# A gated cross-attention block with experts: side work moved from ScalarE's PSUM ring to a two-bank slot of VectorE's ring

## The reference

```
x = x + tanh(g_xattn) * attention(layernorm(x), ctx)   # x 2048 x 256, ctx 1601 x 256, 8 heads of 4 dims
    q = xn Wq + bq; k = ctx Wk + bk; v = ctx Wv + bv    # 256 -> 32
    attn = softmax(q k^T * scale); o = attn v; return o Wo + bo
x = x + tanh(g_ffn) * experts(layernorm(x))             # 8 experts, each takes its 512 best rows
    scores = softmax(xn router_w + router_b); G, idx = top_k(scores.T, 512)
    y[idx] += G * (relu(xn[idx] w1 + b1) w2 + b2)       # 256 -> 1024 -> 256
```

## Time and profile before

| | |
|---|---|
| median of 3 runs | 588.16 us (587.49 to 588.36) |
| the profiled execution | 587.38 us, span 585.6 us |
| granted TensorE clock | 0.996 of full speed |
| busy share of the span | PE 94%, PEld 55%, DVE 76%, ACT 67%, POOL 37% |

### The profile page before, as it was taken

The page is one execution under the profiler, slowest core; times in us unless marked ns, Lnnn a source line. Parts: engine busy times, 40 slices in busy tenths (PEclk is TensorE's granted clock), DMA queues, the critical chain, the costliest instruction groups (busy, mean ns, idle before and its releaser), DMA issues.

```text
span 585.6 us, 12822 instructions
## 1 busy us (share of the span) xinstructions
PE 548.6 (94%) x5043; PEld 319.9 (55%) x5043; DVE 442.3 (76%) x811; ACT 390.1 (67%) x762; POOL 215.0 (37%) x205
## 2 busy tenths in 40 slices
PE   7798999999999999999999988899999999999994
PEld 4433333343343333433334444479889898898973
DVE  3889889987999878999895277655866858676541
ACT  2577778987789887898889820055665556565651
POOL 3058085001835017300184110231544625437234
PEclk9999999999999999999999999999999999999998
DMA  7700000000000000000000105113635646356123
GB/s 275 252 2 1 1 1 3 2 2 37 2 37 2 2 37 1 38 2 2 37 37 2 38 19 163 31 52 107 137 110 107 166 133 136 110 108 164 18 35 36
DMA packets 23808, 35.80 MB, mean 61 GB/s; under 512 B 3460, under 2 KB 16197, under 8 KB 23621
## 3 DMA queue, kind: packets, MB, share of 16 engines
q1 hardware_dynamic: 17604, 26.59, 14.0%
q0 software_dynamic: 6144, 8.39, 8.2%
HBM read 26.59 MB, written 8.39 MB: 60 GB/s over the span
## 4 chain that ended last, share of the span: by engine, by line
PE 69%; DVE 18%; issue 4%; ACT 4%; POOL 1%; DMA 1%; POOLq 0%; DVEq 0%; ACTq 0%; SPq 0%
PE ps L1744 15%; PE ps L1751 15%; PE ps L1515 12%; DVE mquart L1040 11%; PE ps L1481 7%; PE ps L1502 6%; PE ps L1411 2%; ACT probs L767 2%; PE ps L1372 2%; PE ps L1387 1%; PE ps L1722 1%; PE ps L1697 1%; ACT osb L666 1%; PE ps L1540 1%; POOL out L636 1%
## 5 line engine op out<-in xcount | busy, mean ns | idle before, releaser
L1040 DVE TENSOR_REDUCE mquart<-ps 128x2 f32<-128x802 f32 x256 | 240.3, 987 | 27.4 <-PE ps L1481 25.2
L767 ACT ACTIVATE probs<-ps 128x512 f32<-128x512 f32 (+1 forms) x416 | 223.4, 595 | 28.8 <-PE ps L1502 26.2
L1515 PE MATMUL ps<-probs,vp 128*32 128x256 f32 (+1 forms) x1664 | 132.7, 391 | 4.2 <-ACT osb L666 4.0
L1481 PE MATMUL ps<-kpad,qrows 64*128 64x401 bf16 x512 | 89.5, 337 | 6.8 <-DVE mquart L1040 6.4
L1502 PE MATMUL ps<-qfull,kpad 64*128 64x256 bf16 (+1 forms) x832 | 88.6, 272 | 1.6 <-ACT x L788 1.4
L1340 DVE TENSOR_TENSOR h1l<-hf,h1h 128x512 fp32r<-128x512 f32 x64 | 44.2, 691 | 56.2 <-ACT hf L892 54.3
L891 ACT ACTIVATE h1h<-ps,b1T 128x512 fp32r<-128x512 f32 x64 | 44.0, 687 | 54.1 <-PE ps L1744 52.3
L1751 PE MATMUL ps<-w2h,h1h 128*128 128x256 f32 x256 | 73.8, 288 | 2.1 <-DVE h1l L1340 1.5
L1751 PE MATMUL ps<-w2l,h1h 128*128 128x256 f32 x256 | 72.4, 283 | 0.0
L1751 PE MATMUL ps<-w2h,h1l 128*128 128x256 f32 x256 | 72.3, 282 | 0.0
L636 POOL DMA_INDIRECT out<-eo,idx_put x32 | 55.3, 1727 | 26.4 <-ACT eo L901 17.3
(11 more groups left out here) (200 smaller groups left out, 690.4 us busy)
## 6 DMA issues: line engine op xcount, KB each, us to landing
w1raw<-in_L_ffn_w SPq DMA_DIRECT2D x16, 512.0 KB, 4.9
w2raw<-in_L_ffn_w SPq DMA_DIRECT2D x16, 512.0 KB
xs<-in_x SPq DMA_DIRECT2D x4, 512.0 KB, 8.2
ctx_sb<-in_ctx SPq DMA_DIRECT2D x3, 512.0 KB, 6.3
out<-xs SPq DMA_DIRECT2D x3, 512.0 KB, 2.7
x_rows<-x SPq DMA_DIRECT2D x3, 512.0 KB, 2.6
b2b<-in_L_ffn_b SPq DMA_DIRECT2D x1, 1024.0 KB, 10.7
out<-xs SPq DMA_DIRECT2D x2, 256.0 KB, 2.0
```

What stands on the lines that cost most here:

```text
L767: nc.scalar.activation(out_p, ps[0:w, next_bank(), :], ACT.Exp, scale=float(SCALE)).then_inc(s_ex, 1)
L1040: nc.vector.tensor_reduce(mquart[:, u % 2, t, a, :, kq], ps[:, b:b + 2, 0:MAXW], AX.X, ALU.max).then_inc(s_mr, 1)
L1481: last = mm(ps[:, bank + b, 0:MAXW], qrows[band(b), g, q:q + P], kpad[band(b), g, a, lo:lo + MAXW], start=True, stop=True)
L1515: last = mm(ps[32 * hh:32 * hh + 32, PV, 0:UW], vp[0:w, kt, g, hh, :], probs[0:w, step % PROBS, hh, :], start=(kt == 0), stop=(kt == NKT - 1))
```

## The change

The output projection and the turns of both norms leave ACT's ring. PE takes one two-bank slot of DVE's ring for both halves, writes them one after the other at one key tile, and one ACT instruction over 1024 columns takes both. DVE skips the slot in its own count. `slot_bank` works out for ACT which slot it is. The statistics of the norms move to other key tiles. The wait of `add_wo` counts one take for a chunk in place of two.

```diff
-        XN_FIRST, XN_LATER, Q_AT = ((0, 7), (0, 9)), ((0, 0), (0, 3)), ((1, 3), (1, 7))
-        X2_AT, ROUTER_AT = ((2, 7), (2, 9)), ((2, 10), (3, 0))
+        XN_FIRST, XN_LATER, Q_AT = (0, 9), (0, 3), ((1, 3), (1, 7))
+        X2_AT, ROUTER_AT = (2, 9), ((2, 10), (3, 0))
...
-        LN1_AT = {(u, kt): (c, ts) for c, u in ((2, 1), (3, PER_CHUNK + 1)) for kt, ts in ((7, (0, 1)), (8, (2, 3)))}
-        LN1_DONE = {(1, 9): 2, (PER_CHUNK + 1, 9): 3}
-        LN2_AT = {3: (0, 1), 4: (2, 3)}
+        LN1_AT = {(1, 3): (2, (0, 1)), (1, 7): (2, (2, 3)), (PER_CHUNK, 3): (3, (0, 1)), (PER_CHUNK, 9): (3, (2, 3))}
+        LN1_DONE = {(1, 8): 2, (PER_CHUNK, 10): 3}
+        LN2_AT = {3: (0, 1), 7: (2, 3)}
...
+        def dve_slots(u, kt):
+            c, g, h, r = unit(u)
+            return [name for name, here in (("o", (r, kt) == O_THIS), ("o_last", c > 0 and (r, kt) == O_LAST),
+                                            ("wo", c > 0 and (r, kt) == WO_AT), ("xn", c + 1 < NC and (r, kt) == xn_at(c)),
+                                            ("x2", c > 0 and (r, kt) == X2_AT)) if here]
+
+        def slot_bank(u, kt, name):
+            sides = sum(len(dve_slots(v, k)) for v in range(u + 1) for k in range(NKT if v < u else kt))
+            return dve_bank(tiles_by(u, 2 * kt + 1) + sides + dve_slots(u, kt).index(name))
...
-                nc.scalar.activation(x2[:, odd:CT:2, :], ps[:, bank, :].rearrange("p (t d) -> p t d", d=D), ACT.Copy,
+                nc.scalar.activation(x2[:, :, :].rearrange("p (t o) d -> p o t d", o=2),
+                                     ps[:, bank:bank + 2, :].rearrange("p o (t d) -> p o t d", d=D), ACT.Copy,
                                      scale=tg[:, 0:1]).then_inc(s_wt, 1)
...
-            def take_X(c, k, bank):
-                act.wait_ge(s_X, KD * c + k + 1)
-                take(x2T[:, k, :], ps[:, bank, :], s_Xt)
+            def take_X(c, bank):
+                act.wait_ge(s_X, KD * (c + 1))
+                nc.scalar.activation(x2T[:, :, :], ps[:, bank:bank + KD, :], ACT.Copy).then_inc(s_Xt, KD)
...
+                    for name in dve_slots(u, kt):
+                        if name in ("wo", "xn", "x2"):
+                            next_bank()
...
-                    if c > 0 and (r, kt) == (1, 5):
+                    if c > 0 and (r, kt) == (1, 8):
                         ln2_aggr(c - 1)
...
-                        even = next_act((s_wt, 2 * (c - 1) + 1))
-                        wo(c - 1, range(CT), (even, next_act((s_wt, 2 * c))))
-                    if c + 1 < NC and (r, kt) in xn_at(c):
-                        k = xn_at(c).index((r, kt))
-                        transpose_xn(c + 1, k, next_act((s_Tt, KD * (c + 1) + k + 1)))
+                        even = next_dve((s_wt, c))
+                        wo(c - 1, range(CT), (even, even + 1))
+                    if c + 1 < NC and (r, kt) == xn_at(c):
+                        first = next_dve((s_Tt, KD * (c + 2)))
+                        for k in range(KD):
+                            transpose_xn(c + 1, k, first + k)
...
-                    if c > 0 and (r, kt) in X2_AT:
-                        k = X2_AT.index((r, kt))
-                        transpose_x2(c - 1, k, next_act((s_Xt, KD * (c - 1) + k + 1)))
+                    if c > 0 and (r, kt) == X2_AT:
+                        first = next_dve((s_Xt, KD * c))
+                        for k in range(KD):
+                            transpose_x2(c - 1, k, first + k)
```

More of the change, by code:

```diff
@@ L514, in add_wo @@
                 pool.wait_ge(s_xb, c + 1)
-                pool.wait_ge(s_wt, 2 * (c + 1))
+                pool.wait_ge(s_wt, c + 1)
                 rows = xs[:, CT * c:CT * c + CT, :]
@@ L781, in q_full, with scale_wo @@
                 take(qfull[:, g, UW * h:UW * h + UW], ps[:, next_bank(), 0:UW], s_qf)
-            def scale_wo(c, odd, bank):
+            def scale_wo(c, bank):
                 act.wait_ge(s_W, c + 1)
@@ L816, in take_L, with take_xn @@
                 take(lg[:, CT * c:CT * c + CT, :], ps[:, bank, 0:P].rearrange("p (t j) -> p t j", j=32)[:, :, 0:E], s_lgr)
-            def take_xn(c, k, bank):
-                act.wait_ge(s_T, KD * c + k + 1)
-                take(xnT[:, k, :], ps[:, bank, :], s_Tt)
+            def take_xn(c, bank):
+                act.wait_ge(s_T, KD * (c + 1))
+                nc.scalar.activation(xnT[:, :, :], ps[:, bank:bank + KD, :], ACT.Copy).then_inc(s_Tt, KD)
             q_full(0)
@@ L835, in _ @@
                     if c > 0 and (r, kt) == WO_AT:
-                        for odd in range(2):
-                            scale_wo(c - 1, odd, next_bank())
-                    if c + 1 < NC and (r, kt) in xn_at(c):
-                        take_xn(c + 1, xn_at(c).index((r, kt)), next_bank())
+                        scale_wo(c - 1, slot_bank(u, kt, "wo"))
+                    if c + 1 < NC and (r, kt) == xn_at(c):
+                        take_xn(c + 1, slot_bank(u, kt, "xn"))
                     if c + 1 < NC and (r, kt) in Q_AT:
@@ L843, in _ @@
                         qk_bias(n, k, "q", k, CW, next_bank(), s_Q, NG * (c + 1) + k + 1)
-                    if c > 0 and (r, kt) in X2_AT:
-                        take_X(c - 1, X2_AT.index((r, kt)), next_bank())
+                    if c > 0 and (r, kt) == X2_AT:
+                        take_X(c - 1, slot_bank(u, kt, "x2"))
                     if c > 0 and (r, kt) == ROUTER_AT[0]:
```

## The result

| | before | changed |
|---|---|---|
| median | 588.28 us (22 runs) | 587.43 us (22 runs) |
| ratio to before | | 0.9987, 95% interval 0.9981 to 0.9993 |
| profiled execution, span | 585.6 us | 586.8 us |
| from unit 0's first scores to the last exponential | 288.19 us | 287.61 us |

What follows compares the result with a forecast made beforehand. PE's order was taken to bound units with side work, DVE the plain units and unit 0. Terms -1.2 + 1.1 + 0.7 + 0.7 - 1.3 summed to 0.0; with 0.2 off, 588.0 us, range 585.5 to 590.4.

Steps and rivals of the forecast that it cites:

- projection, units 4, 8, 12: Key tile 9: PE's 0.72 us loss behind the projection ends, less a 0.13 slot wait and 0.2 lag; gain 0.4 each.
- first norm's turns, units 4 and 8: Key tile 3: PE stands 0.70 us for the slot ACT is reading; cost 1.88 in place of 1.33, 0.55 slower each.
- first norm's turns, unit 0: Key tile 9: DVE is the bound there and idles 0.68 us behind the turns, not given back; 0.7 slower.
- second norm's turns, units 6, 10, 14: Key tile 9: the router waits for the whole take, 0.15 us in units 6 and 10, 0.4 in 14; 0.7 slower.
- statistics: Moved into DVE's gaps or under cover, mainly in units 1, 5 and 9, they delay PE less; 1.3 us faster together.
- Units with side work are PE-bound: Except in unit 0, PE's own order bounds units with side work (18 to 20.6 us), so edits are priced by PE's stalls.
- the sign: Units 4 and 8 stay at 19.8 to 20.0 us, with PE idle about 0.7 before a maximum, ended by ACT's take.
- POOL's cover: Unit 13's aggregation reaches POOL some 4 us later, hidden by POOL's 7.5 us wait for the last maxima.
- Takes: ACT's single takes last 1.01 us for 1024 columns and 1.10 for the projection.
- the faster one: Whole kernel: PE's stalls are made up at later waits and the covers hold; -2.6 us, 585.5; chance 0.28.
- The slower one: Whole kernel: DVE's queue falls to one maximum and takes start late behind ACT's exponentials; +3.0 us, 591.2; chance 0.17.
- That the statistics give nothing: Rival: the time the statistics held up goes to the wait for a slot; 0 in place of -1.3, 589.3; chance 0.10.

Runs made afterwards that it cites:

- stats_only: The kernel before with only the statistics moved to their new key tiles; ratio to before 0.9967, attention part 286.87 us against 288.19.
- stats_back: The changed kernel with the statistics of both norms back at their old key tiles; ratio to before 1.0012, attention part 288.98 us.
- xn_at_2: The changed kernel with the first norm's turns of units 4 and 8 at key tile 2 instead of 3; ratio to before 0.9980, attention part 287.26 us.
- wo_split: Projection in the slot and statistics moved, turns as before, projection's matmuls bank by bank with two takes; ratio to the kernel before 0.9946, attention part 285.73 us.

## Why the prediction was right, and by which terms

The forecast was 588.0 in a range of 585.5 to 590.4, on the scale of a 588.16 median; measured were 587.43 beside 588.28. That is right in sum. By terms, from the units' lengths in the kernels with one part each:

| step | forecast, us | measured, us |
|---|---|---|
| projection, units 4, 8, 12 | -1.2 | -1.52 |
| first norm's turns, units 4 and 8 | +1.1 | +0.8 |
| first norm's turns, unit 0 | +0.7 | +0.3 |
| second norm's turns, units 6, 10, 14 | +0.7 | +1.2 |
| statistics | -1.3 | -1.32 |
| sum | 0.0 | -0.54 (changed kernel: -0.58) |

- **Units with side work are PE-bound**: right, but for key tile 8 of unit 14 (below). Unit 4 took 1.4 us of DVE work more or less without moving, and PE's stalls came out in the unit's length, less what waits behind them gave back.
- **Projection**: the mechanism was right, its size 0.1 a unit too small. I took 0.2 back for ACT's lag. It is there: key tile 11 goes from 1.39 to 1.70, where the second score pair waits for an exponential (the 0.70 at 282.66). But key tiles 9 and 12 are each 0.1 shorter; at key tile 9 the projection starts 1.07 us behind the scores (279.06 in unit 12), where it was 1.17, since it no longer has to find two of ACT's three banks free.
- **First norm, units 4 and 8**: key tiles 0 to 4 went from 7.19 to 7.74 us, the forecast +0.55. The two errors in it cancelled: eight transposes in a row hold PE for 1.03 and not 1.18, and the stall is 0.84, not 0.70, because ACT's take begins 1.19 after the first transpose, 0.16 later than PE goes on, where I had counted 0.03. What I left out is that key tiles 5 and 6 then get 0.13 back, where PE had waited for DVE. So the units stood at 19.70, just under the 19.8 to 20.0 that I had named as the sign.
- **First norm, unit 0**: DVE's hole is 0.57, against 0.68 forecast, and half of that reached the unit's end. I read the eight maxima of the earlier trace rows as a full DVE. They were not: the changed kernel reads seven in 6.38 us and five in 4.59, a new one each 0.90 us, where those eight took 0.95 each. The merged row hid places where a maximum came late, with 0.08 and 0.07 us of idle time that it doesn't print, the first of them behind the turn at key tile 7. Against one each 0.90 us they had cost 0.36 over the eight; the hole of now costs 0.65 by the same count, and the difference of 0.3 is what the unit lost. The changed kernel's rows, DVE's timeline at the end of unit 0:

```profile
56.90 6.38 DVE L1052 TENSOR_REDUCE mquart<-ps 128x2 f32<-128x802 f32 x7
63.85 0.99 DVE L1052 TENSOR_REDUCE mquart<-ps 128x2 f32<-128x802 f32 x1 [0.57 <-PE ps L1496]
65.28 4.59 DVE L1052 TENSOR_REDUCE mquart<-ps 128x2 f32<-128x802 f32 x5
```

- **Second norm**: the step that was most too small. The router's wait adds 0.4 to key tile 10 in units 6 and 10 where I had 0.15. PE goes on 1.03 after the first transpose and not 1.18, so it reaches the router that much earlier and waits that much longer for a take that ends at 2.2 either way (and it starts 0.15 behind the take's end, not 0.06); key tiles 7 to 9 are 0.17 shorter, which leaves 0.26 a unit. In unit 14 it adds 0.5, and 0.34 more come at key tile 8, where DVE, no longer held off by a turn at key tile 7, is the bound (PE waits 0.16 for it at 313.13); the forecast has nothing there. Both waits in unit 14:

```profile
313.13 0.34 PE L1496 MATMUL ps<-kpad,qrows 64*128 64x401 bf16 x2 [0.16 <-DVE mquart L1052]
314.87 1.09 PE L1562 MATMUL ps<-cst,x 128*128 128x128 f32 x8
317.23 0.64 PE L1578 MATMUL ps<-x2T,rw_pad 128*32 128x128 f32 x16 [0.37 <-ACT x2T L814]
316.06 1.02 ACT L814 ACTIVATE x2T<-ps 128x1024 f32<-128x1024 f32 x1 [0.57 <-PE ps L1562]
```

- **Statistics**: right in each unit: 0.4 in unit 1, 0.8 in unit 5, 0.16 in unit 9, 0 in units 4 and 13. POOL's cover held as well: its wait for the last maxima shrank from 7.5 to 2.9 us and is not gone.
- **Takes**: 1.02 and 1.11 us (1024 and 1115 ns), where my slope gave 1.01 and 1.10. An estimate from the figures of the Trainium skill ("ScalarE: Activation LUTs", section "What ACT_TABLE_LOAD costs") was 1.04 and 1.13; the measurement lies between, nearer the slope.
- **The rivals**: the faster one wanted most stalls made up; 0.13 a unit was. The slower one wanted ACT at exponentials when a side ends; ACT waited 0.56 and 0.73 for PE there, so it never came into play. That the statistics give nothing is refuted by stats_only and stats_back. One thing in the working doesn't hold: it says that the range reaches to both outer cases, but it ends at 590.4 and the slower case at 591.2.

The result is the balance of terms of up to 1.5 us, so its closeness says less than the table does, and part of it is luck: the first three terms were each 0.3 to 0.4 too high and the second norm's 0.5 too low.

What stays open: in xn_at_2 ACT's take began 1.46 after the first transpose in unit 8, and 1.18 in unit 4, with the same rows on PE before it; behind the last transpose's modelled end that is 0.37 against 0.09. With two takes both units start at 0.69. No run here tells why.

## What to carry to other kernels

Joining two takes into one instruction saves 0.06 us at a turn and 0.15 at the projection here, but makes the first half wait for the second; where a slot or a reader hangs on the take, two instructions that follow the producer gave back 0.26 to 0.43 us a place in the changed kernel (nothing in unit 0) and 0.64 at key tile 2. That holds only where the first half is done early: the projection's two banks filled side by side, and there two takes cost 0.13. Price a side job by the producer's time plus the way from the take's end to each thing behind it: the next use of its slot, its reader, and the in-order work queued behind it on the taking engine; the last of these is why one take lost to the old turns at key tile 6 and added 0.3 at key tile 2. Put work of an engine with slack where the bounding engine is busy with something long (0.75 us of statistics were free behind a projection or a turn, and cost 0.46 without one), and time each part of a bundle alone: two of the three parts together are 0.57% faster than before, all three 0.13%.

## What was not expected of the hardware

- Matmuls of 32 rows on two row bands run side by side even when all of one band are issued first (wo_split): they start in pairs 0.01 us apart, the eight end 1.14 after the first by the trace's modelled ends, and a take of one band's bank starts no earlier.
- After the last of eight transposes ACT's take begins 0.10 us behind its modelled end (unit 8 of the changed kernel), and 0.16 after PE's next instruction has started.
- Back to back, a reduction of 802 columns comes every 0.90 us though each lasts 0.99. The eight of the earlier trace rows came every 0.95 and had holes that no row prints.
